# A two-layer graph network over a dense adjacency: rows 0 and 1 in parts, another order of block products

## The reference

```python
h = jnp.maximum(_layernorm(x, axis=-1), 0.0)
x = x + adj @ (h * (u >= 0.1) / 0.9)        # layer 1
h = jnp.maximum(_layernorm(x, axis=-1), 0.0)
x = x + (adj @ (h @ W) + b)                 # layer 2
```

## Time and profile before

| | |
|---|---|
| median of 3 runs | 886.44 us |
| the profiled execution | 886.64 us |
| its span | 884.8 us |
| PE busy | 865.8 us, 98% |
| vector engine (DVE) busy | 564.6 us, 64% |
| DMA | 361.62 MB, 409 GB/s over the span |
| instructions | 13364, of which 5484 matmul and 5484 weight loads |

### The profile page before, as it was taken

One profiled execution on the slowest core, in us unless ns is written; L12 is line 12 of the kernel. 1 busy time (PEld: TensorE's weight loads), 2 busy tenths in 40 slices (PEclk: granted clock), 3 DMA queues, 4 the chain that ended last, 5 costly groups with the idle time before them and its releaser, 6 DMA issues.

```text
span 884.8 us, 13364 instructions
## 1 busy us (share of the span) xinstructions
PE 865.8 (98%) x5484; PEld 490.0 (55%) x5484; DVE 564.6 (64%) x1193; ACT 42.6 (5%) x120; POOL 1.4 (0%) x11
## 2 busy tenths in 40 slices
PE   6799999999999999999999999999999999999998
PEld 5445444444445464465547576666757655567543
DVE  5364633323244548586868686978778898798724
ACT  3100000000000000000000000000000000000000
POOL 0000000000000000000000000000000000000000
PEclk9999999999999999999999999999999999999999
DMA  9999999999999999999999999999999999999993
GB/s 374 420 420 419 422 421 421 420 420 421 422 390 420 421 420 421 418 421 421 419 421 419 420 420 416 416 420 405 420 412 414 392 410 420 419 422 419 418 419 114
DMA packets 52316, 361.62 MB, mean 409 GB/s; under 512 B 5792, under 2 KB 6048, under 8 KB 10016
## 3 DMA queue, kind: packets, MB, share of 16 engines
q1 hardware_dynamic: 52096, 360.73, 98.8%
q10 hardware_dynamic: 160, 0.03, 0.0%
HBM read 358.65 MB, written 2.10 MB: 408 GB/s over the span
## 4 chain that ended last, share of the span: by engine, by line
PE 83%; DMA 10%; DVE 4%; SPq 2%; issue 1%; ACT 0%; DVEq 0%
PE banks L790 30%; PE banks L816 22%; PE row_sums L765 17%; DMA blocks<-in_adj 10%; PE banks L784 6%; PE row_sums L822 5%; PE banks L800 3%; SPq L469 2%; DVE acc L659 0%; PE banks L917 0%; DVE quarters L635 0%; PE banks L884 0%; DVE quarters L631 0%; DVE blocks L633 0%; DVE x L584 0%
## 5 line engine op out<-in xcount | busy, mean ns | idle before, releaser
L790 PE MATMUL banks<-blocks,features 128*64 128x512 f32 x1248 | 379.7, 593 | 0.3 <-DMA blocks<-in_adj 0.3
L765 PE MATMUL row_sums<-blocks,features 128*64 128x512 f32 x984 | 241.8, 592 | 0.6 <-DMA blocks<-in_adj 0.5
L790 PEld LDWEIGHTS banks<-blocks,features 128*64 128x64 f32 x1248 | 128.3, 137 | 134.3 <-issue 131.9
L673 DVE TENSOR_TENSOR acc<-acc,banks 128x512 f32<-128x512 f32 (+1 forms) x106 | 72.6, 685 | 140.1 <-PE banks L790 128.7
L816 PE MATMUL banks<-quarters,mixed 128*64 128x256 f32 x664 | 157.6, 379 | 0.4
L765 PEld LDWEIGHTS row_sums<-blocks,features 128*64 128x64 f32 x984 | 93.0, 137 | 104.6 <-issue 99.0
L784 PE MATMUL banks<-blocks,features 128*64 128x512 f32 x272 | 119.7, 592 | 0.2 <-DMA blocks<-in_adj 0.2
L816 PEld LDWEIGHTS banks<-quarters,mixed 128*64 128x64 f32 x664 | 90.6, 137 | 27.5 <-DVE quarters L641 2.1
L816 PE MATMUL banks<-quarters,features 128*64 128x256 f32 x332 | 85.4, 380 | 0.0
L816 PE MATMUL banks<-blocks,features 128*64 128x256 f32 x332 | 85.3, 379 | 0.1
L822 PE MATMUL row_sums<-blocks,mixed 128*64 128x256 f32 x332 | 85.3, 379 | 0.0
(11 more groups left out here) (63 smaller groups left out, 594.8 us busy)
## 6 DMA issues: line engine op xcount, KB each, us to landing
blocks<-in_adj SPq DMA_DIRECT2D x337, 1024.0 KB, 13.7
x<-in_x SPq DMA_DIRECT2D x2, 1024.0 KB, 7.3
acc<-in_u SPq DMA_DIRECT2D x2, 1024.0 KB, 9.4
out<-x SPq DMA_DIRECT2D x7, 256.0 KB, 2.3
blocks<-in_adj SPq DMA_DIRECT2D x2, 512.0 KB, 26.5
out<-x SPq DMA_DIRECT2D x2, 128.0 KB, 1.8
w_twice<-in_wb ACTq DMA_DIRECT2D x2, 16.2 KB, 6.0
```

What stands on the lines that cost most here:

```text
L673: nc.vector.tensor_tensor(mine, mine, banks[at, q.bank, :], ALU.add).then_inc(sum_added, 1)
L765: return nc.tensor.matmul(row_sums[at, t.unit % 2, nodes], features[:, tile_of(k, j), 0:D], tile, start=start, stop=last and t.n == unit_l ...
L790: return nc.tensor.matmul(banks[at, t.sum.bank, nodes], features[:, tile_of(t.k, j), D:2 * D], tile, start=t.n == t.sum.first and j == t.t ...
```

## The change

Row 0 is cut into three parts (tiles 0, 1, 2-3: 128, 128 and 256 nodes) and row 1 into two (256 and 256), 19 units in all. A `left` load holds as many columns of a part as fill a block: 4, 4, 2 for row 0, 2 and 2 for row 1. The words are now `h`, `i`, `j` for the parts of row 0 and `k`, `l` for those of row 1 (`hK` covers columns K to K + 3, `jK` K and K + 1); `t`, `u`, `v` for the parts of column 0 and `w`, `x` for those of column 1, where `tP` is an item for both rows of pair P, layers 1 and 2, its layer 1 summed in a second bank (`sum_x`). `top` loads hold 4, 4 and 2 rows of column 0, 2 rows of column 1. Parts that another load holds are skipped (`skipped`), so that some first loads are 0.5 or 0.75 of a block. Layer 2 of row 0 takes three products a tile, of row 1 two. A reload of row 0 is two transfers, its first with runs of 2 KB; a reload of row 1 has runs of 4 KB. From row 3 on the order of kept pairs, reloads and sevens is another; there are 42 `r` (41 before), 83 sevens (83), 6 `a` (19), 98 `o` (112). The packing of `adj` on the host follows this. The core of the diff (in the order text only the new lines):

```diff
-HALVES = 2
-HALF_BLK = BLK // HALVES
-HALF_TILES = TILES // HALVES
-UNITS = BLOCKS + 1
+HALF_BLK = BLK // 2
+HALF_TILES = TILES // 2
+SPLIT = [[range(0, 1), range(1, 2), range(2, TILES)], [range(0, 2), range(2, TILES)]]
+WHOLE = [range(TILES)]
+UNIT = [(i, tiles) for i in range(BLOCKS) for tiles in (SPLIT[i] if i < len(SPLIT) else WHOLE)]
+UNITS = len(UNIT)
+FIRST_UNIT = [min(m for m in range(UNITS) if UNIT[m][0] == i) for i in range(BLOCKS)]
 PAIRS = BLOCKS // 2
+GROUP = [[TILES // len(tiles) for tiles in parts] for parts in SPLIT]
+AT = [[sum(BLOCKS // GROUP[i][q] for q in range(part)) for part in range(len(SPLIT[i]))] for i in range(len(SPLIT))]
...
 ORDER = """
+h4 h8 h12 h0 i4 i8 t0 t1 t2 t3 t4 t5 i12 i0 t6 t7 j14 j12 u0 u1 u2 u3 j10 j8 j6 u4 j4 j2 u5 j0 u6 u7 k4 v0 v1 v2
+v3 k6 k8 v4 k10 k12 k14 k2 k0 v5 v6 v7 m0.4 w1 l6 w2 l8 w3 l10 w4 l12 l14 w5 l2 l0 w6 w7 o2.6 x1 p0.1 o2.7 o2.8
+x2 o2.9 o2.10 x3 o2.11 o2.12 x4 o2.13 o2.14 x5 o2.15 o2.5 x6 o2.4 o2.3 x7 o2.2 o3.7 o3.8 o3.9 o3.10 o3.11 o3.12
+m2.6 p0.2 b3.2 o3.13 o3.14 o3.15 o3.5 o3.4 o3.3 o4.8 o4.9 a14.2 a11.2 o4.10 a10.2 a15.2 o4.11 o4.12 o4.13 o4.14
+o4.15 p0.3 o4.7 o4.6 s4.3 p2.3 s4.2 o4.5 o4.4 o5.9 o5.10 a13.2 o5.11 p2.4 o5.12 o5.13 o5.14 m4.8 s5.4 o5.15 s5.3
+a12.2 o5.7 s5.2 o5.6 o5.5 o6.10 o6.11 o6.12 o6.13 o6.14 o6.15 o6.9 p4.5 o6.8 s6.2 s6.5 s6.3 s6.4 o6.7 o6.6 p2.5
+o7.11 o7.12 o7.13 o7.14 s7.4 m6.10 s7.2 s7.5 s7.3 s7.6 o7.15 o7.9 o7.8 o7.7 p4.6 o8.12 r0.5 o8.13 o8.14 o8.15
+o8.11 s8.4 s8.7 o8.10 s8.3 s8.6 o8.9 s8.2 o8.8 s8.5 r2.7 p6.7 o9.13 o9.14 o9.15 p4.7 s9.8 s9.2 s9.5 o9.11 m8.12
+s9.4 o9.10 s9.3 s9.6 o9.9 s9.7 o10.14 r0.8 o10.15 o10.13 p6.9 r2.6 s10.7 r4.8 s10.3 s10.6 s10.8 o10.12 s10.4
+o10.11 o10.10 s10.9 s10.5 r0.9 o11.15 r2.9 p8.10 o11.13 s11.5 s11.8 s11.7 r4.9 s11.3 s11.6 s11.10 r0.4 m10.14
+s11.9 s11.4 o11.12 o11.11 p8.9 o12.15 r2.10 r0.7 o12.14 o12.13 s12.11 o12.12 s12.7 s12.5 s12.10 s12.8 p6.8 s12.6
+s12.4 s12.9 s12.3 r0.6 p8.11 r6.11 p10.12 o13.14 s13.8 r2.8 s13.4 s13.10 s13.11 m12.15 s13.3 s13.5 s13.12 r6.12
+s13.7 s13.9 o13.13 s13.6 r2.12 r2.11 o14.15 r0.11 r8.12 s14.8 s14.5 r4.12 o14.14 s14.10 s14.12 s14.11 s14.9
+p10.11 r6.10 s14.7 s14.6 s14.4 s14.3 s14.13 r6.13 r4.10 p12.13 p10.13 m14.15 s15.10 s15.9 s15.12 r0.12 b15.14
+s15.11 r0.13 p12.14 r4.13 r4.11 s15.4 s15.5 s15.7 r2.13 r8.14 r10.14 s15.6 s15.13 r0.10 s15.8 r8.13 s15.3 r6.14
+r4.14 r2.14 r0.14 p14.15 p12.15 r10.15 r8.15 r6.15 r4.15 r2.15 r0.15
 """
...
+    def __init__(self, kind, i, k, part=0):
+        self.kind, self.i, self.k, self.part = kind, i, k, part
+        self.skipped, self.size = 0, 1.0
+        if kind in ("left", "top"):
+            group = GROUP[i][part]
+            self.skipped = max(0, (i if kind == "left" else i + 1) - k * group)
+            self.size = 1 - self.skipped / group
+        self.transfers = 2 if kind == "again" and i == 0 else 1
...
+        if kind == "ahead":
+            self.steps = len(tiles) * len(operands)
+        if kind == "one" and operands[0][1][0].kind == "left":
+            self.steps = 2 * operands[0][1][0].size
+        self.needs = next(m + 1 for m in range(UNITS) if UNIT[m][0] == k and UNIT[m][1].stop >= tiles.stop)
...
-            t.sum = Sum(t.row // 2, t.row % 2, n)
-            t.sum.ahead = t.row
+            both_rows = len(t.operands) == 2
+            t.sum = Sum(t.row // 2, None if both_rows else t.row % 2, n)
+            t.sum.ahead = None if both_rows else t.row
             sums.append(t.sum)
+            if both_rows:
+                t.sum_x = Sum(t.row // 2, None, n)
+                t.sum_x.of_x, t.sum_x.last = True, n
+                sums.append(t.sum_x)
...
+                if load.kind in ("left", "top"):
+                    of = (left_0, left_1)[i] if load.kind == "left" else (top_0, top_1)[i]
+                    at = load.skipped * len(SPLIT[i][load.part]) * BLK
+                    to, of = blocks[:, slot, at:], of[AT[i][load.part] + k, :, at:]
                 elif i == 0:
-                    to = blocks[:, slot, :].rearrange("p (h c) -> p h c", h=HALVES)
-                    of = adj[0:BLOCKS].rearrange("(h a) p (b c) -> a b p h c", h=HALVES, b=2)[k // 2, k % 2]
+                    at, n = 2 * P * TILES, GROUP[0][0]
+                    to = blocks[:, slot, 0:at].rearrange("p (h c) -> p h c", h=2)
+                    of = left_0[0:AT[0][2]].rearrange("(h a) p (b c) -> a b p h c", h=2, b=n)[k // n, k % n]
+                    sp.dma_start(to, of).then_inc(block_arrived[slot], 16)
+                    n = GROUP[0][2]
+                    to, of = blocks[:, slot, at:], left_0[AT[0][2] + k // n, :, k % n * at:(k % n + 1) * at]
+                elif i == 1:
+                    n = GROUP[1][0]
+                    to = blocks[:, slot, :].rearrange("p (h c) -> p h c", h=2)
+                    of = left_1.rearrange("(h a) p (b c) -> a b p h c", h=2, b=n)[k // n, k % n]
                 else:
-                    to, of = blocks[:, slot, :], adj[i * BLOCKS + k, :, :]
+                    n = len(SPLIT)
+                    to, of = blocks[:, slot, :], adj[(i - n) * (BLOCKS - n) + k - n, :, :]
...
+            def layer_1_of_part(t, load, q, half, last):
+                wide, (column, j) = width(t.unit), divmod(q, TILES)
+                start, started[t.unit, half] = not started[t.unit, half], True
+                return nc.tensor.matmul(row_sums[half * D:(half + 1) * D, t.unit % 2, 0:wide],
+                                        features[:, tile_of(load.k * GROUP[load.i][load.part] + column, j), 0:D],
+                                        blocks[:, load.slot, q * wide:(q + 1) * wide],
+                                        start=start, stop=last and t.n == unit_last[t.unit][half],
+                                        skip_group_check=True)
+            def products_of(load):
+                return range(load.skipped * TILES, GROUP[load.i][load.part] * TILES)
...
+                for part, (nodes, tile) in enumerate(pieces(operand, t.k, j)):
+                    done = nc.tensor.matmul(banks[at, t.sum.bank, nodes], features[:, tile_of(t.k, j), D:2 * D], tile,
+                                            start=t.n == t.sum.first and j == t.tiles[0] and part == 0,
+                                            stop=t.n == t.sum.last and j == t.tiles[-1], skip_group_check=True)
+                return done
...
-                    pe.wait_ge(xd_ready, t.k // 2 + 1)
+                    pe.wait_ge(xd_ready, (t.k + GROUP[0][m] - 1) // 2 + 1)
...
+                            for operand in t.operands:
+                                layer_1_ahead(t, operand, j, 1 - operand[0] % 2)
+                            for operand in reversed(t.operands):
+                                done = layer_2(t, operand, j, operand[0] % 2)
```

More of the change, by code:

```diff
@@ L155, in ordered @@
             i, k = numbers
-            items.append(Item({"o": "one", "b": "both", "s": "seven"}[kind], [operand(i, k)], k, i, i + 1))
+            items.append(Item({"o": "one", "b": "both", "s": "seven"}[kind], [operand(i, k)], k, i, FIRST_UNIT[i]))
     return items
@@ L176, in plan @@
         assert free[load.slot] < min(later.first for later in loads[n:]), "a block needs a slot that is still held"
-        count[load.slot] += 1
+        count[load.slot] += load.transfers
         load.before, load.arrived = holder[load.slot], 16 * count[load.slot]
@@ L306, in bass_gnn @@
      finals, rests_at) = plan()
-    closing = {q.last: q for q in sums}
+    closing = {q.last: [r for r in sums if r.last == q.last] for q in sums}
     final_of = {p: n for n, p in enumerate(finals)}
@@ L746, in pieces @@
                 i, loads = operand
-                if i:
-                    at = loads[0].offset(i) + (j % HALF_TILES if loads[0].kind == "top" else j) * BLK
+                if loads[0].kind == "top":
+                    tiles, group = SPLIT[k][loads[0].part], GROUP[k][loads[0].part]
+                    at = (i % group * len(tiles) + j - tiles.start) * BLK
                     return [(slice(0, BLK), blocks[:, loads[0].slot, at:at + BLK])]
+                if i >= len(SPLIT):
+                    return [(slice(0, BLK), blocks[:, loads[0].slot, j * BLK:(j + 1) * BLK])]
                 found = []
-                for half in range(HALVES):
-                    at = ((half if loads[0].kind == "again" else k % 2) * TILES + j) * HALF_BLK
-                    slot = loads[half if loads[0].kind == "left" else 0].slot
-                    found.append((slice(half * HALF_BLK, (half + 1) * HALF_BLK), blocks[:, slot, at:at + HALF_BLK]))
+                for part, tiles in enumerate(SPLIT[i]):
+                    wide = len(tiles) * P
+                    if loads[0].kind == "again":
+                        load, at = loads[0], tiles.start * P * TILES + j * wide
+                    else:
+                        load, at = loads[part], (k % GROUP[i][part] * TILES + j) * wide
+                    nodes = slice(tiles.start * P, tiles.stop * P)
```

(9 more changed lines are left out.)

169 lines of the change are left out of this document (67 added, 102 removed).

## The result

**893.12 us** median of 4 runs (891.72 to 894.46), beside 886.43 for the kernel before (4 runs, 886.31 to 886.9): 1.0074 times as long, 95% interval 1.0057 to 1.0091. The forecast of 888.0 us got the sign right and the size wrong, and 893.1 lies outside its range. The profiled execution took 894.23 us, 1.1 us over the median; its span is 892.2.

A forecast was written before the change was run, and what follows sets the result against it. TensorE (98% busy) and DMA were both taken to be at their limit. Waited-away start 0.3, fetches 0.6, short runs 0.25 and narrow products 0.4, 1.6 us rounded, on the 886.44 us median gave 888.0 us, range 883.8 to 891.5.

The forecast's parts named there:

- Step 1: At the start: t0 near 34.7 us, 1.2 us saved there, up to 3.8 us if blocks always arrived in time.
- (c): 128-wide products of row 0: 32 instructions in 1.79 us, +0.4 us for seven row-0 pairs after o12.12.
- third rival: Narrow products take slots of their own on PE, row-0 pairs of 4 us and more: 894.2 us; chance 0.08.
- (a): 896 more instructions, hence 3 more instruction fetches over the DMA engines (47 in all): +0.6 us up to 598 us.
- Step 2: Whether blocks arrive in time: at o12.12, near 598 us, the head start is waited away, 0.3 us later than before.
- (b): Reloads of rows 0 and 1 in shorter runs: 0.05 us for each of five, +0.25 us (0 to 1).
- Step 3: More instructions and smaller pieces: the three costs (a) +0.6, (b) +0.25 and (c) +0.4 us.
- second rival: DMA runs dry at blocks 236 to 250, pauses adding up to more than 5 us: 891 us; chance 0.2.
- first rival: The head start survives because blocks arrive at 2.49 us each and PE sets the pace: 883.0 us; chance 0.2.

The follow-up runs named there:

- e6: e2 with the reloaded blocks of rows 0 and 1 in whole-tile layout, so their products are 512 columns wide, not 128; 889.38 us (1.0031).
- e2: The changed kernel with reloads of rows 0 and 1 each in one transfer of 8 KB runs, from an added array; 888.85 us (1.0035).
- e13: e9 with one item, o8.10, moved from behind o7.15 to behind o7.11; 885.48 us (0.9987 of the kernel before).
- e14: The changed kernel with a worked-out order that spaces each row's first product for vector work; short runs and narrow products kept; 888.93 us (1.0024).
- e5: e1 and e2 together: the changed kernel with three products moved and long-run reloads of rows 0 and 1; 889.72 us (1.0032).
- e7: e6 with another order from o3.7 on, worked out from loads and slots without the vector engine; 1006.14 us.
- e9: e6's long runs and wide products with a second worked-out order behind w7, most vector work included; 888.89 us (1.0024).
- e1: The changed kernel with three words of its order moved (o12.15, o12.14, r0.11); 892.02 us (1.0059).

## Why the prediction was wrong

*Step 1 (start): right.* `t0` at 34.48 for 34.7, the head start 3.3 us where up to 3.8 was possible. *(c) narrow products: right.* The items of 32 narrow instructions on PE follow each other in 1.75 us where not held up (forecast 1.79), 0.055 us an instruction, and nine of the eleven pairs of row 0 in 3.42 to 3.55 us (3.45 before; forecast 3.3 to 3.5). The 81 ns of the Trainium skill (TensorE: Matmul & The Clock Gate, Back-to-back issue gap), which would have made it 2.6, isn't borne out by this trace; e6 excludes the third rival. *(a) fetches:* 48, forecast 47; the prediction counted 224 more products, and there are 244 (976 more instructions of the two kinds, not 896). e6's 544 fewer instructions, two fetches, brought nothing, nearer to the Trainium skill's "mostly hidden" (Runtime: NRT & Kernel Launch, Instruction fetch mechanics) than to my 0.6 us, though 0.6 is close to what the runs can tell.

*Step 2 (stations): right in kind, a little short in size.* The head start was waited away by 660.5 steps, as forecast. PE was 1.7 us behind there, not 0.3, or 1.15 with (a) and (b). The block that decided it was not `o12.12`'s, which landed at 599.28 for 597.8, but `o12.13`'s, at 594.48 for 592.9. With long runs the orders are level there.

***Step 3 (b) is the term that failed, in its size and in its reach.*** "I take 0.05 us for each of five, +0.25 us (0 to 1)". I read one window over a 4 KB reload of before, in which 423 GB/s went by, and took its price for that of 2 KB runs in two transfers. And I took it for the five pairs up to 598 us alone; for the seven behind them step 2 says "PE-bound", so they cost nothing in the sum. Measured: the five pairs were 2.7 us late in all, the seven 7.3; 10.0 us over 24 reloads, and 4.3 us of time. The last block landed at 881.4 us, where the forecast had 871; with long runs (e2) it lands at 873.4. Of the 7.5 us by which the trace ends behind, 5.8 come after 660.5 steps, where the sum had 0.4 of (c). The 11 pairs of before were 1.8 us late in all, eight of them by 0.08 us or less; so 0.05 was a fair reading of a quiet one of those. The fault is that I carried it over to runs half as long and to a second transfer, of which no row of before holds one, where even a quiet pair is 0.2 us late, and left the tail without a term.

***The second rival had the right place and mechanism and the wrong price.*** The forecast put it at nothing. It named blocks 236 to 250 and `r8.12` with 3 us of cover. I counted one stop of 1.5 us, near 630 us. In the trace the four loads ahead of `r0.6`, each freed by a seven, came 3.0 us apart for 2.49, and 25 us at 319 GB/s for 417 are 5.9 us of transfers; 3 us of cover were not enough, and `r8.12` waited 2.59. With long runs the same stretch (share 0.94) leaves a wait of 1.04 us (e2). Its condition ("more than 5 us") was met, its time, 891, was 2.1 us short: no term stood for the clock, which took 1.7 us at `r8.12`. The rows of before could not tell: its clock is full in every slice, and the longest idle times of PE in its start, behind its first instruction, are 1.20 and 1.43 us.

*What the change is worth apart from its order:* the first rival was no fancy. With long runs and an order made for the new start, e13 is 1.2 us under the kernel before, not the 3.4 of the rival. It is 3.2 us ahead of the old order at 150 steps and 1.5 at 215: 1.5 us are lost at `a11.2` (208 us), which waits for row 2's features. From there it keeps all but 0.3.

**Open.** Which of the two, 2 KB runs or the second transfer for one block, makes row 0's reloads late was not tried apart; row 1's, one transfer of 4 KB runs, were late as well (3.4 of the 10.0 us in the changed kernel, 5.2 of e14's 8.4). The long runs also come from an added array; that its place in memory plays no part isn't shown. Why single loads in long runs land late, 2.8 us on a short queue at e5's `s13.4` and 0.9 us and more on full ones, isn't settled either. Nor is why a pair in short runs is late by 0.2 us in most places and by 2 in some.

## What to carry to other kernels

A head start is worth what the next station leaves of it: carry time by step count along both orders, and look where the two lines cross, not at busy shares, which read the same here for kernels 9 us apart. In a kernel bound by loads, a change of layout that shortens runs must be priced at every reload, not in one window. When an order is rewritten, list all that an item waits for (load, slot, features, bank, vector work); each kind left out cost as much as the whole gain sought or more (some 120 us in e7, 3.4 in e9).

## What was not expected of the hardware

A wait of PE can cost more than its length: 1.23 us of idle time (e13) and 1.84 (e6, at `r8.12`) left the clock full (1.00 in the windows after); 2.59 us (0.78 and 0.88 in the windows after) and 2.95 us (0.54 in the window around it, near the lower level of 1.2 GHz) were followed by 1.7 and 3.0 us of extra time. At the start, where PE idles 3.84 and 1.72 us for x, the window from 20 to 25 us is granted 0.51.

DMA can be busy and slow: in e1 a share of 0.98 with 366 GB/s, where 1.01 goes with 417 to 423 elsewhere. The share alone would have called that stretch full.
